# A four-layer graph transformer: products two units behind their turns, and the output projection, residual and statistics of each pair of blocks taken inside the attention loop

## The reference

```python
h = x @ Wn + bn
for l in range(4):
    Q = h @ WQ[l] + bQ[l]; K = h @ WK[l] + bK[l]; V = h @ WV[l] + bV[l]
    scores = jnp.sum(Q[dst] * K[src], axis=-1) * scale
    e = jnp.exp(scores - segment_max(scores, dst)[dst])
    attn = e / segment_sum(e, dst)[dst]
    messages = segment_sum(attn[:, None] * V[src], dst)
    out = messages @ WO[l] + bO[l]
    h = layernorm(h + out, ln_g[l], ln_b[l])
return h @ Wout + bout
```

## Time and profile before

| | us |
|---|---|
| median of 3 runs | 3109.26 (3108.5 to 3112.21) |
| the profiled execution | 3098.46 |
| its span | 3096.7 |
| TensorE busy | 2541.8 (82%) |
| VectorE busy | 2452.3 (79%) |
| ScalarE busy | 1959.3 (63%) |
| a layer of the transformer | about 348, four of them from 1695 on |

### The profile page before, as it was taken

How to read it: one execution, slowest core, us unless ns; L and a number is a source line. 1 busy time by engine, 2 the same in 40 slices (tenths; PEclk the granted TensorE clock), 3 DMA queues, 4 the chain that set the end, 5 groups by cost and what they waited for, 6 DMA issues and landing times. The chain is left out here.

```text
span 3096.7 us, 59422 instructions
## 1 busy us (share of the span) xinstructions
PE 2541.8 (82%) x19197; PEld 2084.3 (67%) x19197; DVE 2452.3 (79%) x5292; ACT 1959.3 (63%) x3958; POOL 219.9 (7%) x487
## 2 busy tenths in 40 slices
PE   0888888867458888888883899979998899979997
PEld 0555555546446666666662788859886798869886
DVE  7999999833579999899977677767776677767776
ACT  1666666621248888788873577747775577757774
POOL 3000000000000000000000111001110111001110
PEclk9999899977669999899996999989999999989998
DMA  1232333373063325432311333314331333314332
GB/s 42 74 130 89 130 120 120 134 243 125 9 180 120 111 105 162 128 125 105 107 64 65 115 143 141 131 43 144 131 143 65 111 143 143 129 44 146 145 127 60
DMA packets 87376, 355.52 MB, mean 115 GB/s; under 512 B 47453, under 2 KB 59541, under 8 KB 59796
## 3 DMA queue, kind: packets, MB, share of 16 engines
q1 hardware_dynamic: 87149, 352.59, 32.7%
HBM read 285.86 MB, written 65.67 MB: 114 GB/s over the span
## 5 line engine op out<-in xcount | busy, mean ns | idle before, releaser
L1844 ACT ACTIVATE awcol<-aturned 125x500 fp32r<-125x500 f32 (+2 forms) x652 | 372.8, 572 | 359.0 <-PE aturned L1761 354.4
L1942 DVE TENSOR_TENSOR awcol<-aturned,awcol 125x500 fp32r<-125x500 f32 (+2 forms) x652 | 428.2, 657 | 156.0 <-ACT awcol L1844 151.0
L1773 PE MATMUL asum<-awcol,vals_high 125*128 125x512 f32 (+1 forms) x1300 | 480.6, 390 | 6.9 <-DVE awcol L1942 4.2
L1366 PE MATMUL gturned<-ident,grow 125*125 125x125 f32 x2500 | 406.5, 304 | 27.5 <-ACT grow L1304 27.5
L1773 PE MATMUL asum<-awcol,vals_low 125*128 125x256 f32 x1300 | 406.2, 321 | 6.6 <-DVE awcol L1942 6.6
L1366 PEld LDWEIGHTS gturned<-ident,grow 125*125 125x125 f32 x2500 | 329.6, 203 | 104.3 <-issue 73.0
L1273 DVE SCALAR_TENSOR_TENSOR grow<-line,a_dst 125x3125 f32<-125x3125 f32 x100 | 347.5, 3475 | 29.7 <-DMA line<-lines_dram 22.5
L1304 ACT ACTIVATE grow<-grow,neg 125x3125 f32<-125x3125 f32 x100 | 290.4, 2904 | 122.7 <-DVE neg L1285 122.7
L1282 DVE CUSTOM_DVE_ANT_0 grow<-grow,bias 125x3125 f32<-125x3125 f32 x100 | 341.6, 3416 | 23.8 <-DMA bias<-bias_dram 9.5
L1344 PE MATMUL gparts<-gwcol,h_mem 125*32 125x125 f32 x5000 | 241.6, 288 | 113.9 <-ACT gwcol L1317 113.9
L1317 ACT ACTIVATE gwcol<-gturned 125x1000 f32<-125x1000 f32 x300 | 281.3, 1001 | 14.5 <-PE gturned L1366 14.4
(11 more groups left out here) (307 smaller groups left out, 4853.3 us busy)
## 6 DMA issues: line engine op xcount, KB each, us to landing
abias<-bias_dram SPq DMA_DIRECT2D x100, 1562.5 KB, 6.5
bias<-bias_dram SPq DMA_DIRECT2D x50, 1562.5 KB, 6.6
bias_dram<-lnrow SPq DMA_DIRECT2D x25, 1562.5 KB, 5.2
counts_dram<-pair SPq DMA_DIRECT2D x13, 1562.5 KB, 6.4
pair<-counts_dram SPq DMA_DIRECT2D x13, 1562.5 KB, 16.1
line<-lines_dram SPq DMA_DIRECT2D x8, 1367.2 KB
fixed<-kp SPq DMA_DIRECT2D x250, 4.0 KB, 1.7
agg<-counts_dram SPq DMA_DIRECT2D x2, 1367.2 KB
```

Of the source, the lines that this page charges most:

```text
L1366: last = pe.transpose(bank[q % RING][:, j // 4, j % 4 * T:(j % 4 + 1) * T], row[n % RING][:, t * T:(t + 1) * T], ident[0:T, 0:T])
L1773: last = pe.matmul(sum_ps[e][:, 0:n_cols], left[:, t, :], buffer[:, j * wide:j * wide + n_cols], start=(t == 0 and n == 0), stop=(t == NT ...
L1844: act.activation(operand(P, e, u, 0), turned(P, e, u), ACT.Copy).then_inc(high_copied, 1)
L1942: dve.tensor_tensor(operand(P, e, u, 1), turned(P, e, u), operand(P, e, u, 0).bitcast(FP32), ALU.subtract).then_inc(low_made, 1)
```

## The change

Six edits, all in `transformer`:

1. Products come two units after their turn, not one; `wcol` has four buffers in place of three. ScalarE's `finish` moves to unit 2, VectorE's to unit 3, as the last product of a pair now ends later.
2. The log counts of block 2 are issued before `load_ahead`, once the first chunk of block 1 is read. The other loads stay behind it.
3. `values` only adds the bias; `vals_low` is taken chunk by chunk in the units of the single block. TensorE waits for V at the single block's unit 0, after that unit's scores.
4. The messages of a pair go to a buffer of their own, `message[e]`. VectorE's `finish` also inverts the pair's denominators and multiplies them by `has_in`.
5. New on TensorE, `out_rows`: at unit 5 (OUT_AT) of the next pair, the output product of the pair's two blocks, into the bank `sum_ps[e]` that the messages came from.
6. New on VectorE, `residual`: at unit 6, the two blocks' residual addition and their statistics, into `parts3`. The output product, the additions and the statistics in `leave` go away.

```diff
-        wcol = [sbo(f"awcol{k}", [T, 2, 2 * HALF], FP32R) for k in range(T_BANKS)]
+        wcol = [sbo(f"awcol{k}", [T, 2, 2 * HALF], FP32R) for k in range(W_BUFFERS)]
...
+                    step(2, 1)
                     banks.done(sp, f"q{l}", NC)
                     banks.done(sp, f"v{l}", NC)
                     load_ahead(l, last)
...
                     with sp.Fori(1, NT // 2) as i:
-                        step(2 * i, 1)
                         step(2 * i + 1, 0)
-                    step(NT - 1, 1)
+                        step(2 * i + 2, 1)
...
+                    def out_rows(P, e):
+                        pe.wait_ge(sum_read, P + (1 + SUMS_AHEAD + PAIRS_OF * l))
+                        for n in range(len(halves(P))):
+                            last = pe.matmul(sum_ps[e][0:T, n * D:(n + 1) * D], message[e][:, n * T:(n + 1) * T], w[:, 3, :], start=True, stop=True)
+                        last.then_inc(out_ready, 1)
...
                             ahead(P, e, u, scores)
+                            if single(P) and u == 0:
+                                banks.done(pe, f"v{l}", NC)
+                            if u == OUT_AT and not single(P):
+                                if isinstance(P, int) and P == 1:
+                                    pe.wait_ge(loaded, ahead_loads(l))
+                                out_rows(P - 1, 1 - e)
                             turn(P, e, u)
-                            if u:
-                                weigh(P, e, u - 1)
+                            if u >= 2:
+                                weigh(P, e, u - 2)
                             elif not single(P):
                                 before = P - 1
-                                weigh(before, 1 - e, units(before)[-1])
+                                weigh(before, 1 - e, units(before)[u - 2])
...
-                    weigh(LAST_PAIR, 0, UNITS - 1)
+                    for u in (UNITS - 2, UNITS - 1):
+                        weigh(LAST_PAIR, 0, u)
+                    out_rows(LAST_PAIR, 0)
...
-                    pe.wait_ge(sum_read, SUMS_AHEAD + PAIRS_OF * (l + 1))
-                    pe.wait_ge(loaded, ahead_loads(l))
-                    pe_rows(pe, banks, f"out{l}", [cols], [w[:, 3, :]])
...
-                        if c:
-                            low_values(c - 1)
-                    chain(dve, post_marks, low_values(NC - 1))
...
+                        dve.wait_ge(exp_done, block_of(P, 1) * NC + (NC + LAYER_CHUNKS * l))
+                        mine = den[:, blocks_of(P)]
+                        made = lambda n: P * 3 + (n + 3 * PAIRS_OF * l)
+                        dve.tensor_reduce(mine.unsqueeze(2), expsum[e][:, 1:2, :] if single(P) else expsum[e][:, :, :], AX.X, ALU.add).then_inc(den_made, 1)
+                        dve.wait_ge(den_made, made(1))
+                        dve.sem_inc(G["passed"], 1)
+                        dve.reciprocal(mine, mine).then_inc(den_made, 1)
+                        dve.wait_ge(den_made, made(2))
+                        dve.sem_inc(G["passed"], 1)
+                        dve.tensor_tensor(mine, mine, G["has_in"][:, blocks_of(P)], ALU.mult).then_inc(den_made, 1)
                         dve.wait_ge(msg_high, P + (1 + PAIRS_OF * l))
                         at = HALF // 2 if single(P) else HALF
-                        dve.tensor_tensor(message(P), message(P), sum_ps[e][:, at:at + width(P)], ALU.add).then_inc(sum_read, 1)
+                        dve.tensor_tensor(message[e][:, 0:width(P)], message[e][:, 0:width(P)], sum_ps[e][:, at:at + width(P)], ALU.add).then_inc(sum_read, 1)
+
+                    def residual(P, e):
+
+                        dve.wait_ge(den_made, P * 3 + (3 + 3 * PAIRS_OF * l))
+                        dve.wait_ge(residual_done, block_of(P, 1) * 2 + (2 + 2 * NT * l))
+                        dve.wait_ge(out_ready, P + (1 + PAIRS_OF * l))
+                        dve.sem_inc(G["passed"], 1)
+                        for n, half in enumerate(halves(P)):
+                            b = bass.ds(block_of(P, half), 1)
+                            last = dve.scalar_tensor_tensor(out=work[:, b, :], in0=sum_ps[e][0:T, n * D:(n + 1) * D].unsqueeze(1), scalar=den[:, b],
+                                                            in1=h[:, b, :], op0=ALU.mult, op1=ALU.add).then_inc(residual_added, 1)
+                        for half in halves(P):
+                            b = block_of(P, half)
+                            dve.wait_ge(residual_added, b + (1 + NT * l))
+                            dve.sem_inc(out_read if half else G["passed"], 1)
+                            made = dve.bn_stats(parts[:, bass.ds(b, 1), :].rearrange("p a d -> p (a d)"),
+                                                work[:, bass.ds(b, 1), :].rearrange("p a d -> p (a d)"))
+                        return made
...
                             ahead(P, e, u, maximum)
+                            if single(P):
+                                low_values(l, u)
                             low_part(P, e, u)
-                            if u == 2 and not single(P):
+                            if u == 3 and not single(P):
                                 finish(P - 1, 1 - e)
+                            if u == OUT_AT + 1 and not single(P):
+                                residual(P - 1, 1 - e)
```

More of the change, by code:

```diff
@@ L1555, in transformer @@
         neg = [sbo(f"aneg{k}", [T, 1]) for k in range(4)]
-        expsum = [sbo(f"expsum{k}", [T, NC]) for k in range(4)]
+        expsum = [sbo(f"expsum{k}", [T, 2, NC]) for k in range(2)]
+        message = [sbo(f"message{p}", [D, 2 * T]) for p in range(2)]
         s_ps = [ps(f"scores{k}") for k in range(S_BANKS)]
@@ L1561, in transformer @@
         for l in range(LAYERS):
-            stages += [(f"k{l}", NC, "dve"), (f"q{l}", NC, "act"), (f"v{l}", NC, "dve"), (f"out{l}", NC, "dve"), (f"normed{l}", NC, "act")]
+            stages += [(f"k{l}", NC, "dve"), (f"q{l}", NC, "act"), (f"v{l}", NC, "dve"), (f"normed{l}", NC, "act")]
         stages += [("node_out", NC, "dve")]
@@ L1576, in transformer @@
         owner = ["act" if t in (3, 7, 11, 15) else "dve" for t in range(NT)]
-        norms = [Norm(sem, "norm", stat, work, h, spare, relu=False, turn=l) for l in range(LAYERS)]
+        norms = [Norm(sem, "norm", stat, work, h, parts, relu=False, turn=l) for l in range(LAYERS)]
         v_whole = x
@@ L1629, in turned, with blocks_of @@
             return turned_ps[slot(P, e, u)][0:T, 0:len(tiles(P, u)) * width(P)].rearrange("p (t d) -> p t d", d=width(P))
[L1631 to L1632 removed]
+        def blocks_of(P):
+            return slice(0, 1) if single(P) else bass.ds(P * 2 - 1, 2)
         with nc.Block() as block:
@@ L1844, in step @@
                             act.activation(operand(P, e, u, 0), turned(P, e, u), ACT.Copy).then_inc(high_copied, 1)
-                            if u == 1 and not single(P):
+                            if u == 2 and not single(P):
                                 finish(P - 1, 1 - e)
@@ L1964, in attend @@
                     finish(LAST_PAIR, 0)
+                    chain(dve, post_marks, residual(LAST_PAIR, 0))
                 def leave(l):
-                    dve.wait_ge(sum_read, SUMS_AHEAD + PAIRS_OF * (l + 1))
-                    chain(dve, post_marks, dve.reciprocal(den[:, :], den[:, :]))
-                    chain(dve, post_marks, dve.tensor_tensor(den[:, :], den[:, :], G["has_in"][:, :], ALU.mult))
-                    dve.wait_ge(residual_done, 2 * NT * (l + 1))
-                    for c in range(NC + 1):
-                        if c < NC:
-                            ts = tiles_of(c)
-                            bank = banks.full(dve, f"out{l}", c)
-                            for j, t in enumerate(ts):
-                                end = dve.scalar_tensor_tensor(out=work[:, t, :], in0=bank[0:T, j * D:(j + 1) * D], scalar=den[:, t:t + 1],
-                                                               in1=h[:, t, :], op0=ALU.mult, op1=ALU.add)
-                            end.then_inc(banks.read["dve"], 1)
-                        if c:
-                            banks.done(dve, f"out{l}", c)
-                            for t in tiles_of(c - 1):
-                                end = norms[l].tile_statistics(dve, t)
-                    chain(dve, post_marks, end)
                     norms[l].scales(dve, post_marks)
```

41 lines of the change are left out of this document (22 added, 19 removed).

## The result

The changed kernel takes 3007.43 us (median; 3000.12 to 3009.49) against 3108.88 for the kernel before (median of four runs): a ratio of 0.967, 95% interval 0.965 to 0.9691. That is faster by 101.5 us.

The account below looks back on a forecast made before the run. TensorE was taken as the bound in steady pairs, waits at layer starts and last pairs, VectorE in the tail. Terms -39 + 5 - 9 - 44 = -87 us, off the median 3109.26 (rounded terms -86): 3023 us, range 3008 to 3048.

Parts of the forecast that it names:

- The steady pair: Loop, 44 pairs: a 0.35 us wait goes, output product adds 0.46; net +0.11 a pair, +5 us, ends 2 and 10.
- The message: Steady pair, VectorE to TensorE's unit 5: message ready about 0.6 us before TensorE wants it, so no wait.
- Rival 1: Message comes late, TensorE stops at unit 5: 0.4 us in 44 pairs adds 18, 3041 us; chance 0.13.
- The last pair: Each layer's last pair, without scores: low-part waits go, output product added; gain 2.3 us a layer, -9 us, ends -12 and -4.
- The start: First value product to pair 1's scores: two TensorE waits go, layers 0 to 2 reach 24.0 us; -39 us, ends -42 and -30.
- rival 5: Start: loads still land late as SP waits for something else; 4.4 + 1.4 us of three layers missing, 3040 us; chance 0.03.
- Rival 2: VectorE, with 21.65 us of work, bounds the start; only half of its gain comes, 3042 us; chance 0.10.
- The tail: First out product to norm's first statistic: 12.69 us falls to 1.8; 10.9 a layer, -44 us, ends -45 and -40.
- rival 3: Tail: shorter idle keeps the clock up, 25 transposes run at 2.4 GHz; gain 1.5 us a layer, 3017 us; chance 0.06.

## What the prediction had right, and the steps that failed

**Which engine bounds which stretch** was right everywhere: TensorE's own work in a steady pair, waits at both ends of a layer, VectorE in the tail. What failed is the size of two terms, the start first and the loop next, and each lay outside its own ends.

**The steady pair.** Forecast 23.3 us, measured 23.21; VectorE busy 19.3 forecast, 18.97 measured. The two terms were each off a little in the same direction. The wait of one place was sized at 0.35 us where its own sum had left 0.4 unexplained, and the kernel with edits 1 to 3 alone shows 0.41. `out_rows` was taken at 0.46 and measures 0.42 to 0.44. Here are the unit and its neighbours in the changed kernel's chain, start, length, what; compare:

```profile
2122.23 0.70 PE asum L1783 x4
2122.93 0.68 PE scores L1759 x3
2123.60 0.44 PE asum L1791 x4
```

The difference per pair is 0.1 us, but 44 pairs make it 4.7 us, over a third of the whole miss. The low end of this term (+2) was also above the measured +0.3.

**The message.** Forecast: ready 0.6 us before TensorE wants it, no wait. VectorE in order of time, the same pair:

```profile
2121.07 0.68 DVE L1961 TENSOR_TENSOR awcol<-aturned,awcol 125x500 fp32r<-125x500 f32 x1
2121.66 0.16 DVE L1969 TENSOR_REDUCE den<-expsum 125x14 f32 x1
2121.97 0.17 DVE L1972 RECIPROCAL den<-den  x1
2122.36 0.16 DVE L1975 TENSOR_TENSOR den<-den,has_in  x1 [0.22 <-DVE den L1972]
2122.47 0.41 DVE L1978 TENSOR_TENSOR message<-message,asum 128x250 f32<-128x250 f32 x1
```

TensorE at that message, its first weight load and its first product:

```profile
2123.22 0.18 PEld L1791 LDWEIGHTS asum<-w,message 128*125 128x125 f32 x1
```
```profile
2123.44 0.38 PE L1791 MATMUL asum<-w,message 128*125 128x128 f32 x2
```

The message ends at 2122.88. The weight load that reads it starts at 2123.22 and the product at 2123.44, so it is early by 0.3 to 0.6 us, and there is no wait. The chain from the low part's end to the message takes 1.13 us against 1.2. The small reciprocal takes 0.17 us, not the 0.3 taken from the 25-element one. The Trainium skill ("VectorE: DVE Perf Modes", The TRN2 errata) states its formula for an fp32 `tensor_tensor` addition; applied to the reciprocal it gives an estimate of 0.16 us for two elements, and that was nearer. Rival 1 did not come true in any steady pair, and the kernel with `out_rows` at unit 4 shows that it would have at one unit less.

**The last pair.** The forecast was -9, the comparable number is -11.1, and it hides two errors of opposite sign. The kernel with edits 1 to 3 alone shows what two-late products give there: 22.71 - 19.27 + 0.71 = 4.15 us a layer, where 2.8 was forecast (2.7 + 0.6 - 0.5). What was sized too small is the restart, 0.07 us a wait. In the kernel before, seven products a layer wait in the last pair, and each starts 0.56 us later than one that doesn't wait, of which the list shows 0.32: that is 3.9 us a layer, with 1.7 of it outside the list. Against that, `out_rows` costs 1.37 a layer and not 0.5, since the units of the last pair have no scores between them, unit 5 comes sooner, and the message isn't there: rival 1 was true in this one step. The prediction had weighed the message's slack only in a pair with scores. Taking it two units later there gave 0.94 of it back.

**The start: the step that failed.** The forecast was 24.0 us a layer, and the comparable number is 21.87 + 0.71 = 22.6; the gain was -44.2 us, outside the ends of -42 and -30. Two numbers of the step were too high:
- The floor, "25.7 - 2.6 = 23.1". 25.69 is TensorE's busy time in a window where it restarts twice, and the half clock taken off was itself too small: half of the 3.1 us that the prediction reads at 0.50 is 1.5, not 1.3. The second stretch at that level, from the restart on, in the kernel before:

```profile
2085.34:2088.20 2.86, 2.86 (x10) 2.59 (x11) 2.41 (x7) 0.37 (x1) 1.57 (x4) 0.50 0.61 171
```

  The two halves are 3.0 us and give 22.7. The kernel without later low parts is busy 21.27 us, all of its stretch; with the 0.71 that is 22.0. The last 0.7 of the difference is not explained. A sum of the work by durations from undisturbed rows, as for the steady pair, comes out right: 25 value tiles at 0.22, 14 score chunks (8 at 0.68, 6 at 0.51), 25 transposes at 0.11 and 44 products of 256 columns at 0.12 are 22.1 us. The floor was 1.1 us too high in each layer.
- The 0.9 us added for VectorE. The kernel with low parts taken once shows 0.6. An engine that is 91% busy was taken for nearly a bound; here it runs three chunks behind, and TensorE hardly waits for it.

Together 1.4 us in four layers, the 5 us of the term. The mechanism was right in both waits. What it had wrong was the price of one wait by itself: rival 5 put the late loads at 17 us, and put back alone they cost 40.9. The early low parts put back alone cost 19.5. Together the two account for a start that is 47.0 us shorter. Rival 2 (3042) was false, and rival 5 too: the load leaves ahead of the small ones. SP's queue in layer 1 (start, length, what), compare:

```profile
2045.89 0.35 SPq L1663 DMA_DIRECT2D abias<-bias_dram  x1
2052.71 0.35 SPq L1649 DMA_DIRECT2D w<-in_L_gnn_WO  x1
```

The issue at 2045.89 is that of block 2, 0.2 us before the first value product, where the forecast had it just before the first value product too (2060.6 against 2060.83).

**The tail.** Forecast -44, measured -42.6. The step from the last message to the norm, changed kernel, all engines in order of time:

```profile
2339.61 0.70 PE L1791 MATMUL asum<-w,message 128*125 128x128 f32 x4 [0.92 <-DVE message L1978]
2340.57 0.61 DVE L1988 SCALAR_TENSOR_TENSOR q_mem<-asum,den,h_mem 125x128 f32<-125x128 f32 x2 [1.01 <-PE asum L1791]
2341.10 0.52 DVE L1994 BATCH_NORM_STATS2 parts<-q_mem 125x6 f32<-125x128 f32 x2
2341.66 0.20 DVE L98 TENSOR_TENSOR stat<-parts 125x25 f32<-125x25 f32 x1
```

From the first product (2339.61) to the norm's first operation (2341.66) pass 2.05 us, forecast 1.8. The missing 0.25 is the way from product to VectorE: it starts 0.96 us after the product does, where 0.5 for the products and a share of 0.2 for semaphores had been put. TensorE's idle fell to 4.4 us as forecast (4.3), and the transposes stayed at half clock (0.53 on average), so rival 3 was false for this kernel.

**The rest.** The -1.4 us in the last row of the table are a matter of when the clock comes back, and chance rather than the change. Layers 0 to 2 take 0.7 us more than before, and the stretch behind the last statistic takes 20.75 us against 22.84. The final product of the kernel ran at 0.57 before and at 1.00 after (`node_out`, a stretch of each):

```profile
3084.00:3089.00 5.00, 5.00 (x26) 5.00 (x27) 1.38 (x2) 0.00 (x0) 0.00 (x0) 0.57 0.21 51
```
```profile
2997.00:3001.00 4.00, 3.95 (x36) 3.95 (x37) 2.22 (x4) 0.00 (x0) 0.00 (x0) 1.00 0.26 64
```

The kernels with the output product at unit 4, with the low parts first and with the low parts once have the same code there as the changed kernel, and take 22.1 to 22.8 us, as the kernel before does; the two others that have it, products one unit late and late log counts, take 20.8 to 20.9. So these 2.1 us differ between executions of the same code, and a difference of 1 to 2 us between two stages shows nothing. What sets the level was not tried.

**The sum.** Of the 12 us between -87 and -99.1, the start gives 5.2, the loop 4.7, the last pair 2.1, the rest 1.4, and the tail takes 1.4 back. The range was too narrow at its low end because the ends of two terms, start and loop, excluded what happened, each by its own sizing error. To take the difference off the median and not off the profiled execution was right: the latter had begun this stage earlier than any other execution seen.

**What undoing doesn't add up to.** One unit late costs 50.6, late counts 40.9, early low parts 19.5, and dropping edits 4 to 6 costs 19.8. That is 130.8 for a change that gave 99.1. Edits 1 to 3 are worth more with the others in place (edit 1 12.7 us a layer against 8.4; in each of layers 0 to 2, edit 2 11.6 against 7.5 and edit 3 4.9 against 0.7). Edits 4 to 6 without the first three were not run.

## What to carry to other kernels

Cost a stretch whose waits will go by its instructions at undisturbed durations, not by its busy time, which here held a lower clock and more: 25.7 us for 22.0 of work. Read what a wait costs from one start to the next, not from the list of waits. Before pieces of work are moved into a full loop, look at the order on the in-order engine that will carry them: in this kernel it wasn't the sum of its work that made a neighbour wait but the burst, and a second unit between turn and product made the burst free. Check a wait's slack in the first and last iteration apart from the steady one, as they have less work between the same two events.

## What the runs showed of the hardware

- A wait costs more than the idle time that the profile lists for it. At one place 0.53 us were lost from start to start and 0.29 listed (products one unit late); there 23.0 us of listed waits came with 50.6 us of lost time, and with the output product at unit 4 61.8 us came with 74.3. The four products behind such a wait take 0.80 us against 0.78, so they are not slower themselves.
- Idle of 4.4 us ahead of the normed transposes leaves them at 0.53 of the clock on average, the lower level of 1.2 GHz for most of them. With 34 dummy transposes in it, TensorE's only work there, the granted clock is 1.00 throughout, and the stretch takes 22.45 us where kernels without them take 23.3 to 24.9. "TensorE: Matmul & The Clock Gate", Part 1, of the Trainium skill says that an idle stretch throttles the array; the trace with the idle agrees, and in the one without it the clock does not fall.
- VectorE was busy for 91% of a stretch of 21.87 us; with 2.35 us of its work gone the stretch was only 0.6 shorter.
- Identical code ahead of the transformer ended between 1695.0 and 1711.6 us in ten profiled executions. This is more than the effect of several of the edits here.
